# Maxima of the self attention's first group moved from the attention loop into the program before it

## Chip, cores and metric

One Trainium2 chip, one core in use. The metric is the device time of one execution in microseconds (us), median of several runs. The profile is that of one further execution.

## What is computed

The reference is a decoder of two post-normalised layers on `x` of 4 x 512 x 256. The part that matters here is the seam between the routed expert layer of layer 0 and the self attention of layer 1:

```python
x = _layernorm(x + _L0_ffn_ref(x, ...))            # 16 experts, top 1, plus a shared expert
x = _layernorm(x + _L1_attn_ref(x, L1_attn_wq_w, ...))
# _L1_attn_ref: 4 batches of 512 rows, 16 heads of 16 columns
q = apply_rope(x @ wq_w + wq_b); k = apply_rope(x @ wk_w + wk_b); v = x @ wv_w + wv_b
scores = einsum('bnqh,bnkh->bnqk', q, k) / sqrt(16)
scores = where(causal, scores, finfo.min)
attn = softmax(scores); ctx = einsum('bnqk,bnkh->bnqh', attn, v); out = ctx @ wo_w + wo_b
```

## The kernel before

**The combining program** (`combine_and_prepare`, from L1504) has 13 steps `c`. In steps 0 to 7 it adds the experts' outputs and normalises a chunk of x; in steps 2 to 9 the chunk is transposed; from step 4 on each step makes one pair of blocks: q or k of one batch, 128 columns by 512 rows each (16 blocks `n`, four for a batch, q before k). A block is projected by PE (L1591), rotated by DVE in two instructions of two parts (`dve_rot`, L333 and L334), added by POOL (`pool_whole`, L353) and then split in three bf16 parts, since the scores are made from bf16 products: ACT rounds it (`act_hi`, L318), DVE takes the rest (`dve_rest`, L342), ACT rounds that (`act_mid`, L325), POOL makes the third part (`pool_lo`, L358), and SP stores the parts to the HBM tensors `qs` and `ks` (L368). After the k blocks of a batch PE makes its values (L1599), ACT copies them (`val.act_copy`, L517) and SP stores them to `vs` (L523). Step 10 makes the q blocks of the last batch (12 and 13), step 11 its k blocks (14 and 15, called REST). DVE's list in a step is: rotate this step's blocks, then the rests of the step before. The splitting of blocks 14 and 15 and the stores of blocks 12 to 15 and of the last batch's values (`keys.late`) are left to the next program. SP loads Q and K of the first three groups of heads (`sa_Q`, `sa_K`) before the stores of blocks 6, 8 and 10.

**The attention loop** (`heads_loop(..., "sa", ...)`, from L1778) runs over 16 groups of 4 heads of one batch, with a ring of R = 5 buffers. For each group:
- phase 1: 16 units (head, 128 query rows). PE makes the scores of one unit (L1992) in one of 3 PSUM banks; DVE adds the causal mask and takes the row maximum into `mx` in one instruction (L2136), which frees the bank. 
- shift: DVE splits the maxima in two bf16 parts (`high` L2149, `low` L2153), PE turns them (L2001), DVE copies them to `mrow` (L2157), and two small DMAs of SP (`maxima`, L1878) put them as two more rows under Q. This stands behind unit 3 of the next group.
- phase 2: PE makes the transposed scores with the shift included (L2016, pairs of heads, two PSUM pair-banks), ACT takes Exp (L2091), POOL cuts the triangle (L1928), PE multiplies with the values (L2032), ACT copies the output (L2081).

The order on PE is: 16 units of group 0; 16 units of group 1, with shift(0) behind unit 3; then phase 2 of group 0, with the 16 units of group 2 strewn in, and so on: phase 2 of group g runs with phase 1 of group g+2. In the first group, units 0 to 4 of group 2 and shift(1) stand before the third pair of scores. DVE makes the two rests of blocks 14 and 15 behind units 4 and 6 of group 1. ACT waits for the landing of the last value store before its first Exp.

The order on SP in the loop is: stores of blocks 12 and 13; `maxima(0, 0)`; stores of block 14; value store and store of block 15; `stored` (a wait for all of these); loads of Q and K of groups 3 and 4; `maxima(1, 1)`; reload for group 5; `maxima(2, 2)`; and so on.

Of the kernel before, what the change touches and what calls it, by code (L numbers as in the profile page):

```python
# [27 lines left out]
F32 = mybir.dt.float32  # L28
BF16 = mybir.dt.bfloat16
I32 = mybir.dt.int32  # L30
ALU = mybir.AluOpType
ACT = mybir.ActivationFunctionType
AX = mybir.AxisListType.X

P = 128
B, L, D = 4, 512, 256
N = B * L
T = N // P
TB = L // P
# [9 lines left out]
G = 4  # L49
# [1454 lines left out]
def combine_and_prepare(nc, env, hT, xs, slot, hb):  # L1504
# [14 lines left out]
    with ExitStack() as c_:  # L1519
# [10 lines left out]
        def dst(n):  # L1530
# [5 lines left out]
        sp_ = Split(env, c_, "sqk", L, bias, dst, lambda n: [SLOTS[blocks[n][1]]], 4, homes=lambda n: HOMES[blocks[n][1]],  # L1536
                    rope=lambda n: (env.cos, env.sin_neg if blocks[n][2] == 0 else env.sin))

        pair = lambda item: PS[:, (4 + 2 * (item % 2)) * BANK:(6 + 2 * (item % 2)) * BANK]
        item_of = lambda n: 3 * (n // 4) + n % 4 // KD  # L1540

# [4 lines left out]
                pe.wait_ge(val.s_v, b + 1) if what == 2 else sp_.freed(pe, 4 * b + KD * what + 1)  # L1546

        def store(sp, n):
            if n % 4 == 3:
                val.sp_out(sp, n // 4)  # L1550
            sp_.sp_out(sp, n)

        with nc.Block() as block:

            @block.gpsimd
            def _(pool):
                def gather(c):
                    for t in PAIR_TILES(c):
                        pool.indirect_dma_start(out=xs[:, t, :], out_offset=None, in_=env.yg,
                                                in_offset=bass.IndirectOffsetOnAxis(ap=slot[:, t:t + 1], axis=0)  # L1560
                                                ).then_inc(s_ga[c], 16)

                for c in range(AHEAD):
                    gather(c)
                for c in range(STEPS):
                    if c < CHUNKS:
                        tail.pool_rstd(pool, c)
                    if c + AHEAD < CHUNKS:
                        gather(c + AHEAD)
                    for n in blocks_at(c):  # L1570
                        sp_.pool_whole(pool, n)
                    for n in blocks_at(c - 1):
                        if n not in REST:
                            sp_.pool_lo(pool, n)

            @block.tensor
            def _(pe):
                pe.sem_inc(tail.s_proj, DONE)
                for c in range(STEPS):
                    if DONE <= c < CHUNKS:  # L1580
                        tail.pe_proj(pe, c, lambda k: w["f_wd"][:, k, :],
                                     lambda i, k: hT[:, k, (2 * c + i) * P:(2 * c + i + 1) * P])
                    if 2 <= c < CHUNKS + 2:
                        tail.pe_out(pe, c - 2)
                    for n in blocks_at(c):
                        b, name, m = blocks[n]
                        if m == 0:
                            pe.wait_ge(tail.s_xT, TB // 2 * (b + 1))
                            item_free(pe, item_of(n))
                        for k in range(KD):  # L1590
                            last = pe.matmul(pair(item_of(n))[:, m * L:(m + 1) * L], w["s_w" + name][:, k, m * P:(m + 1) * P],  # L1591
                                             env.xT[:, k, b * L:(b + 1) * L], start=(k == 0), stop=(k == KD - 1))
                        last.then_inc(sp_.s_full, 1)
                        if n % 4 == 3:
                            item_free(pe, 3 * b + 2)
                            for j in range(TB):
                                t = b * TB + j
                                for k in range(KD):
                                    last = pe.matmul(pair(3 * b + 2)[:, j * D:(j + 1) * D], env.xT[:, k, t * P:(t + 1) * P],  # L1599
                                                     w["s_wv"][:, k, :], start=(k == 0), stop=(k == KD - 1))  # L1600
                            last.then_inc(val.s_full, 1)

            @block.scalar
            def _(act):
                for c in range(STEPS):
                    if 2 <= c < CHUNKS + 2:
                        tail.act_out(act, c - 2)
                    if len(blocks_at(c - 1)) and blocks_at(c - 1)[-1] % 4 == 3:
                        b = blocks_at(c - 1)[-1] // 4
                        val.act_copy(act, b, pair(3 * b + 2))  # L1610
                    for n in blocks_at(c - 1):
                        if n not in REST:
                            sp_.act_mid(act, n)
                    for n in blocks_at(c):
                        if n not in REST:
                            sp_.act_hi(act, n, None)

            @block.vector
            def _(dve):
                val.init(dve)  # L1620
                for c in range(STEPS):
                    if c < CHUNKS:
                        u = c % tail.ring
                        tail.dve_sum(dve, c, biased=False)
                        dve.wait_ge(tail.s_r, c + 1)
                        dve.wait_ge(s_ga[c], 16 * 2)
                        dve.tensor_tensor(tail.r[:, u, :, :], tail.r[:, u, :, :], xs[:, 2 * c:2 * c + 2, :],
                                          ALU.add).then_inc(s_all, 1)
                        tail.dve_stats(dve, c, ready=s_all)
                    if 1 <= c <= CHUNKS:  # L1630
                        tail.dve_apply(dve, c - 1)
                    for n in blocks_at(c):
                        m = blocks[n][2]
                        ps = pair(item_of(n))
                        sp_.dve_rot(dve, n, n - m + KD, ps[:, m * L:(m + 1) * L], ps[:, (1 - m) * L:(2 - m) * L])
                    for n in blocks_at(c - 1):
                        if n not in REST:
                            sp_.dve_rest(dve, n)

            @block.sync  # L1640
            def _(sp):
                def load(g):
                    hb.load_q(sp, g, g)
                    hb.load_k(sp, g, g)

                for n in range(LATE):
                    if n == LOADS[0]:
                        sp_.sp_end(sp, 4)
                    if n in LOADS:
                        load(LOADS.index(n))  # L1650
                    store(sp, n)

    return LaterKeys(sp_, val, store, range(LATE, len(blocks)), REST)

class LaterKeys:

    def __init__(self, split, val, store, late, rest):  # L1660
        self.split, self.val, self.store, self.late, self.rest = split, val, store, late, rest

    def landed(self, engine, b):

# [7 lines left out]
class HeadBuffers:  # L1672
# [5 lines left out]
    def __init__(self, env, c, name, NK, causal, qp, kp, vp, Q=None):  # L1678
# [3 lines left out]
        sb, _ = env.alloc(c)  # L1682
        self.K = sb(name + "_K", [P, self.RING, G * NK], BF16)
        self.Q = Q if Q is not None else sb(name + "_Q", [P, self.RING, G, L], BF16)

    def grow(self, env, c, name, ring):

# [87 lines left out]
    return units  # L1775

def heads_loop(nc, env, name, hb, OT, keys=None, queries=None):  # L1778

# [10 lines left out]
    cut = [0, NK] if causal else [0, BANK, 2 * BANK, NK - LEFT, NK]  # L1791
    CUTS = len(cut) - 1
    if causal:
        units = [(h + j, qt, 0) for h in range(0, G, 2) for qt in (3, 0, 2, 1) for j in range(2)]
    else:
        units = units_of_cuts(CUTS)
    U = len(units)
    R1 = 3
    EARLY = U if causal else 18
    LEAD = U if causal else 5  # L1800
    TURNS = 3
# [31 lines left out]
    with ExitStack() as c:  # L1833
# [2 lines left out]
        PR = KT if causal else R  # L1836
        Pr = sb(name + "_P", [P, PR, G, L], F32)
        part = sb(name + "_part", [P, 2, COLS, CUTS], F32)
        mx = sb(name + "_mx", [P, 2, COLS], F32)
        mh = sb(name + "_mh", [P, 2, 2, COLS // 2], BF16)  # L1840
        mrow = sb(name + "_mrow", [2 * COLS, P], BF16)
        if R > hb.RING:
# [3 lines left out]
        s_ones = sem(name + "_ones")  # L1846
        s_v = [sem(f"{name}_v{u}") for u in range(R)]
        s_mq = [sem(f"{name}_mq{u}") for u in range(R)]
        s_1 = sem(name + "_1")
        s_1free = sem(name + "_1free")  # L1850
        if not causal:
            s_cuts = sem(name + "_cuts")
            s_mrow = sem(name + "_mrow")
# [13 lines left out]
        with nc.Block() as block:  # L1867

            @block.sync
            def _(sp):  # L1870
# [13 lines left out]
                    hb.load_k(sp, g + R, u)  # L1884

                if causal:
                    for n in keys.late:
                        if n == keys.rest[0]:
                            maxima(0, 0)
                        keys.store(sp, n)  # L1890
                    keys.stored(sp)
                else:
                    hb.load_q(sp, 1, 1)
# [8 lines left out]
                    hb.load_q(sp, u, u)  # L1902
                    hb.load_k(sp, u, u)
                for g in range(GROUPS - 1):
                    maxima(g + 1, (g + 1) % R)
                    if g + R < GROUPS:
                        reload(g, g % R)

# [60 lines left out]
            def _(pe):  # L1969
# [93 lines left out]
                for n in range(U):  # L2063
                    if not causal and n in project_at:
                        block_, k = project_at[n]
                        queries.project(pe, block_, queries.ps(block_), (k,))
                    unit(0, 0, n, 0)
                for n in range(LEAD):
                    unit(1, 1, n, 0)
                    if n == BEHIND:  # L2070
# [7 lines left out]
            def _(act):  # L2078
# [23 lines left out]
                act.sem_inc(s_pv, PR)  # L2102
                act.sem_inc(s_ot, 1)
                if causal:
                    for n in keys.rest:
                        keys.split.act_hi(act, n, None)
                    for n in keys.rest:
# [16 lines left out]
            def _(dve):  # L2124
# [33 lines left out]

                for g in range(GROUPS):
                    for n in range(U):  # L2160
                        unit(g, n)
                        if causal and (g, n) in rest_after:
                            keys.split.dve_rest(dve, rest_after[g, n])
                        if not causal and not g and n in split_after:
# [590 lines left out]
```

## Time and profile before

| | us |
|---|---|
| median of 3 runs | 1492.09 |
| lowest and highest | 1489.83 and 1494.17 |
| the profiled execution, whole | 1491.71 |
| its span | 1489.7 |
| PE busy in the span | 1368.9 |
| DVE busy | 1062.0 |
| ACT busy | 774.5 |
| the combining program's last two steps, up to the loop's first matmul | 619 to 642 |
| the attention loop | 642 to 800 |

The busy time of PE is a poor guide here: matmuls are pipelined and overlap with waiting, and each stage of the kernel has its own limit. The stage to look at is read from the order of time: which engine starts what, and what it had waited for.

### The profile page before, as it was taken

The page shows a single profiled execution, that of the slowest core. Times are in us where ns is not written, and L with a number is a line of the kernel's source. Part 1 is how long each engine was busy: PE and PEld are TensorE (multiplying, and loading weights), DVE is VectorE, ACT ScalarE, POOL GpSimd, SP SyncE. Part 2 cuts the span into 40 slices and gives each one's busy share as a digit, 9 for nine tenths or more (in the row PEclk, how much of TensorE's full clock was granted, in tenths as well). Part 3 has the DMA queues.
Part 4 walks back from the last instruction along what each step waited for, and adds up shares of the span by engine and source line. Part 5 has one row for each costly group of instructions (what it writes and reads, how often), then busy time and mean ns, then how long its engine had stood idle before and what let it go on. Part 6 is the DMA issues. An engine that isn't in the chain of part 4 may idle for free. (4 is left out here: it accounts for less than half of the span.)

```text
span 1489.7 us, 24886 instructions
## 1 busy us (share of the span) xinstructions
PE 1368.9 (92%) x9358; PEld 761.6 (51%) x9358; DVE 1062.0 (71%) x2351; ACT 774.5 (52%) x1066; POOL 322.9 (22%) x407
## 2 busy tenths in 40 slices
PE   6897899989999989858998889999999999999996
PEld 3565578856898877423345422333333333333285
DVE  4887466661121128878994798999999999997077
ACT  2344266621111102326664315787888888888754
POOL 3110322243000017743335440000000000000011
PEclk9999799999999999959999968999999999999999
DMA  9548533356988842774421650333222343220001
GB/s 340 194 139 245 166 122 128 124 171 228 299 274 300 278 143 80 222 216 123 134 76 42 187 171 2 77 98 91 68 67 68 80 100 86 68 67 2 1 1 57
DMA packets 152841, 198.68 MB, mean 133 GB/s; under 512 B 15723, under 2 KB 124799, under 8 KB 152594
## 3 DMA queue, kind: packets, MB, share of 16 engines
q1 hardware_dynamic: 141004, 165.34, 36.9%
q0 software_dynamic: 9200, 29.64, 6.5%
q10 hardware_dynamic: 2518, 2.13, 0.5%
q8 instruction: 74, 1.21, 0.3%
q14 instruction: 45, 0.37, 0.1%
HBM read 136.08 MB, written 60.70 MB: 132 GB/s over the span
## 5 line engine op out<-in xcount | busy, mean ns | idle before, releaser
L2139 DVE TENSOR_REDUCE xa_part<-psum 128x1 f32<-128x512 f32 (+1 forms) x768 | 462.6, 661 | 20.5 <-PE psum L1992 18.6
L2091 ACT ACTIVATE xa_P<-psum 128x1024 f32<-128x1024 f32 (+1 forms) x416 | 403.5, 1020 | 105.4 <-PE psum L2016 104.7
L2016 PE MATMUL psum<-sa_Q,xa_K 48*128 48x512 bf16 (+3 forms) x1664 | 268.1, 382 | 3.9 <-DMA sa_Q<-xa_mrow 2.9
L1992 PE MATMUL psum<-xa_K,sa_Q 48*128 48x512 bf16 (+1 forms) x768 | 239.4, 388 | 4.9 <-DVE xa_part L2139 1.5
L2032 PE MATMUL psum<-xa_P,xa_V 128*32 128x512 f32 (+1 forms) x1664 | 223.5, 609 | 0.4 <-ACT xa_P L2091 0.4
L1992 PEld LDWEIGHTS psum<-xa_K,sa_Q 48*128 48x128 bf16 x768 | 59.3, 94 | 232.1 <-DVE xa_part L2139 160.6
L2016 PEld LDWEIGHTS psum<-sa_Q,xa_K 48*128 48x128 bf16 (+3 forms) x1664 | 105.7, 97 | 69.5 <-ACT xa_P L2091 21.2
L2136 DVE CUSTOM_DVE_ANT_0 psum<-psum,cf_sb 128x512 f32<-128x512 f32 (+3 forms) x256 | 119.4, 521 | 19.3 <-PE psum L1992 18.6
L1334 PEld LDWEIGHTS psum<-xtT,wgu 128*128 128x128 f32 x992 | 115.5, 192 | 5.8 <-issue 4.6
L1334 PE MATMUL psum<-xtT,wgu 128*128 128x128 f32 x992 | 115.9, 275 | 1.4 <-issue 0.8
L2091 ACT ACTIVATE sa_P<-psum 128x1024 f32<-128x1024 f32 (+3 forms) x128 | 83.4, 702 | 43.3 <-PE psum L2016 43.1
L1483 DVE TENSOR_TENSOR ht<-sgt,psum 128x512 f32<-128x512 f32 x31 | 21.3, 687 | 113.4 <-ACT sgt L1386 113.4
L1386 ACT ACTIVATE sgt<-psum 128x512 f32<-128x512 f32 x31 | 18.5, 597 | 132.7 <-PE psum L1334 132.7
L1992 PE MATMUL psum<-sa_K,sa_Q 48*128 48x512 bf16 (+3 forms) x256 | 70.6, 331 | 13.9 <-DVE sa_mx L2136 6.7
L212 POOL TENSOR_TENSOR t_rstd<-t_ve,mhalf 128x2 f32<-128x2 f32 (+1 forms) x36 | 27.6, 767 | 228.3 <-DVE t_ve L207 228.1
L2016 PE MATMUL psum<-sa_Q,sa_K 50*128 50x256 bf16 (+7 forms) x512 | 65.1, 311 | 4.8 <-ACT sa_P L2091 2.5
L1941 POOL CAST xa_mh<-xa_mx 128x16 bf16<-128x16 f32 x16 | 3.2, 198 | 295.0 <-DVE xa_mx L2145 266.9
L2032 PEld LDWEIGHTS psum<-xa_P,xa_V 128*32 128x32 f32 (+1 forms) x1664 | 33.0, 108 | 54.1 <-issue 50.6
L634 PE MATMUL psum<-a_in_sb,xT_sb 128*128 128x384 f32 x128 | 48.4, 525 | 12.6 <-DMA xT_sb<-in_xT 9.9
L1928 POOL TENSOR_SCALAR_AFFINE_SELECT sa_P<-sa_P 128x512 f32<-128x512 f32 x64 | 40.7, 636 | 87.7 <-ACT sa_P L2091 87.7
L1215 PE MATMUL psum<-xT_sb,big_weights 128*128 128x512 f32 x128 | 58.8, 614 | 0.6 <-PEq L937 0.6
L1344 PE MATMUL psum<-wdn,ht 128*128 128x256 f32 x248 | 58.7, 380 | 0.6 <-DVE yt L1490 0.6
(245 smaller groups left out, 2126.2 us busy)
## 6 DMA issues: line engine op xcount, KB each, us to landing
wgu<-in_f_gu SPq DMA_DIRECT2D x31, 1024.0 KB
xa_K<-kx SPq DMA_DIRECT2D x192, 100.1 KB, 5.0
wdn<-in_f_dn SPq DMA_DIRECT2D x31, 512.0 KB
vx<-xv_v SPq DMA_DIRECT2D x48, 256.0 KB, 3.4
xa_V<-vx POOLq DMA_DIRECT2D x16, 768.0 KB, 6.5
sa_Q<-qs SPq DMA_DIRECT2D x64, 96.0 KB, 2.3
sa_K<-ks SPq DMA_DIRECT2D x64, 96.0 KB, 2.4
sa_Q<-qx SPq DMA_DIRECT2D x64, 96.0 KB, 2.3
```

The costliest lines, as they stand in the source:

```text
L212: pool.tensor_tensor(self.rstd[:, u, :], self.ve[:, u, :], self.env.mhalf[:, 0:self.tc], ALU.pow).then_inc(self.s_rstd, 1)
L634: pe.matmul(o, env.xT[:, k, t * P:(t + 1) * P], w["a0_in"][:, k, cols], start=(k == 0), stop=False)
L1215: last = pe.matmul(o, w[name][:, k, f * P:(f + 1) * P], env.xT[:, k, c * L:(c + 1) * L], start=(k == 0), stop=(k == KD - 1))
L1334: last = pe.matmul(GU(j)[:, f * P:(f + 1) * P], wgu[:, u, k, f * P:(f + 1) * P], xtT[:, u, k, :], start=(k == 0), stop=(k == KD - 1))
L1344: last = pe.matmul(Y_PS[:, 0:D], ht[:, u, f, :], wdn[:, u, f, :], start=(f == 0), stop=(f == FC - 1))
L1928: pool.affine_select(square, square, [[0, G], [1, P]], ALU.is_ge, 0.0, base=0, channel_multiplier=-1).then_inc(s_tri, 1)
L1992: last = pe.matmul(out[:, 0:width], hb.q(u)[tile:tile + HALF, to, qt * P:(qt + 1) * P], hb.k(u)[tile:tile + HALF, to, cut[e]:cut[e] + widt ...
L2016: last = pe.matmul(out(j), hb.k(u)[tile:tile + depth, to, kt * P:kt * P + r], hb.q(u)[tile:tile + depth, to, q0(kt):L], start=(half == 0), ...
L2032: last = pe.matmul(O_PS[h * VW:(h + 1) * VW, q0(kt):L], Vg[0:r, u, kt, h * VW:(h + 1) * VW], Pr[0:r, (u * KT + kt) % PR, h, 0:L - q0(kt)], ...
L2091: act.activation(Pr[0:r, (u * KT + kt) % PR, h:h + 2, 0:w_], S_PS(p)[0:r, :, 0:w_], ACT.Exp, scale=SCALE).then_inc(s_exp, 1)
L2136: dve.tensor_tensor_reduce(src[:, 0:k1], src[:, 0:k1], env.later[:, L - k1:L], 1.0, -3e38, ALU.add, ALU.max, mx[:, g % 2, col + qt:col + q ...
L2139: dve.tensor_reduce(part[:, g % 2, col + qt, e:e + 1], src[:, 0:cut[e + 1] - cut[e]], AX, ALU.max).then_inc(s_1free, 1)
```

## The change

- Units 0 to 15 of group 0 are taken out of the loop, on PE and DVE, and put into the combining program as class `FirstMaxima`: units 0 to 7 at the end of PE's list for step 10, units 8 to 15 at the end of step 11 (behind the k blocks and the values). In DVE's list six of the eight stand between the rotations and the rests, two behind the rests. They use PSUM banks 0 to 2 and wait for the tail's transposes to be done, and for the load of group 0.
- `mx` is allocated with the head buffers, and the two semaphores of phase 1 in the combining program.
- SP in the loop: the last batch's value store goes first, ahead of the stores of blocks 12 and 13; `maxima(1, 1)` goes ahead of `stored` and the loads of groups 3 and 4.
- ACT in the loop: a one-element Exp goes first, so that the table of Exp is loaded there.

```diff
@@ combine_and_prepare
+        first = FirstMaxima(env, hb, sem)
+        units_at = lambda c: range((c - CHUNKS - 2) * first.STEP, (c - CHUNKS - 1) * first.STEP) if c in (CHUNKS + 2, CHUNKS + 3) else ()
         def store(sp, n):
-            if n % 4 == 3:
+            if n % 4 == 3 and n // 4 < B - 1:
                 val.sp_out(sp, n // 4)
@@ PE, end of a step
+                    for n in units_at(c):
+                        if n == 0:
+                            pe.wait_ge(tail.s_r, CHUNKS)
+                            pe.wait_ge(tail.s_xT, CHUNKS)
+                        first.pe_unit(pe, n)
@@ DVE, after the rotations
+                    for n in units_at(c)[:first.BEFORE_REST]:
+                        first.dve_unit(dve, n)
                     for n in blocks_at(c - 1):
                         if n not in REST:
                             sp_.dve_rest(dve, n)
+                    for n in units_at(c)[first.BEFORE_REST:]:
+                        first.dve_unit(dve, n)
@@
+CAUSAL_UNITS = [(h + j, qt) for h in range(0, G, 2) for qt in (3, 0, 2, 1) for j in range(2)]
+UNIT_BANKS = 3
+class FirstMaxima:
+    STEP = len(CAUSAL_UNITS) // 2
+    BEFORE_REST = 6
+    def pe_unit(self, pe, n):
+        h, qt = CAUSAL_UNITS[n]
+        if n == 0:
+            pe.wait_ge(self.hb.s_kq[0], 16 * self.hb.LOADS)
+        if n >= UNIT_BANKS:
+            pe.wait_ge(self.s_1free, n - UNIT_BANKS + 1)
+        tile, to, width = base(h), place(h, 0), (qt + 1) * P
+        pe.matmul(self.bank(n)[:, 0:width], self.hb.q(0)[tile:tile + HALF, to, qt * P:(qt + 1) * P],
+                  self.hb.k(0)[tile:tile + HALF, to, 0:width], start=True, stop=True,
+                  tile_position=(tile, 0)).then_inc(self.s_1, 1)
+    def dve_unit(self, dve, n):
+        h, qt = CAUSAL_UNITS[n]
+        dve.wait_ge(self.s_1, n + 1)
+        src, col, width = self.bank(n), h % 2 * G * TB // 2 + h // 2 * TB, (qt + 1) * P
+        dve.tensor_tensor_reduce(src[:, 0:width], src[:, 0:width], self.env.later[:, L - width:L], 1.0, -3e38,
+                                 ALU.add, ALU.max, self.hb.mx[:, 0, col + qt:col + qt + 1]).then_inc(self.s_1free, 1)
@@ heads_loop, SP
                 if causal:
+                    keys.val.sp_out(sp, B - 1)
                     for n in keys.late:
                         if n == keys.rest[0]:
                             maxima(0, 0)
                         keys.store(sp, n)
+                    maxima(1, 1)
                     keys.stored(sp)
@@
                 for g in range(GROUPS - 1):
-                    maxima(g + 1, (g + 1) % R)
+                    if g >= 1 or not causal:
+                        maxima(g + 1, (g + 1) % R)
@@ heads_loop, PE
-                    unit(0, 0, n, 0)
+                    if not causal:
+                        unit(0, 0, n, 0)
@@ heads_loop, ACT
                 if causal:
+                    act.activation(part[0:1, 0, 0, 0:1], env.mhalf[0:1, 0:1], ACT.Exp)
@@ heads_loop, DVE
-                        unit(g, n)
+                        if g or not causal:
+                            unit(g, n)
```

## Rows read from the trace of the kernel before

**Rows 1.** Timeline, outputs of the groups: start, length, engine, line, operation [idle before].
```profile
677.42 0.60 ACT L2081 ACTIVATE OT<-psum 128x512 f32<-128x512 f32 x1
687.90 0.60 ACT L2081 ACTIVATE OT<-psum 128x512 f32<-128x512 f32 x1
696.03 0.60 ACT L2081 ACTIVATE OT<-psum 128x512 f32<-128x512 f32 x1
```
**Rows 2.** Windows: length, busy of PE, PEld, DVE, ACT, POOL, granted clock, DMA share, GB/s.
```profile
622.60:627.20 4.60, 0.00 (x0) 0.00 (x0) 4.28 (x6) 1.74 (x4) 3.97 (x3) 0.77 0.92 266
627.20:632.00 4.80, 4.74 (x6) 2.17 (x7) 0.39 (x1) 1.44 (x3) 2.27 (x2) 0.50 0.95 295
674.90:685.30 10.40, 9.84 (x82) 3.61 (x84) 7.21 (x30) 5.76 (x9) 2.84 (x5) 0.67 0.34 100
685.30:695.50 10.20, 9.46 (x106) 4.08 (x102) 9.73 (x45) 6.98 (x11) 3.68 (x6) 1.00 0.50 139
```
**Rows 3.** Timeline of the combining program's end, and the loop's first matmul.
```profile
618.96 3.60 PE L1591 MATMUL psum<-xT_sb,s_wq_sb 128*128 128x512 f32 x8
...
627.26 6.00 PE L1591 MATMUL psum<-xT_sb,s_wk_sb 128*128 128x512 f32 x8 [4.70 <-ACT sv_v L517]
...
633.10 3.62 PE L1599 MATMUL psum<-s_wv_sb,xT_sb 128*128 128x256 f32 x16
...
635.94 2.35 DVE L342 TENSOR_TENSOR sqk_rest<-sqk_whole,sqk_parts 128x512 f32<-128x512 f32 x2
...
637.70 2.71 POOL L358 TENSOR_TENSOR sqk_parts<-sqk_rest,sqk_parts 128x512 bf16<-128x512 f32 x2
...
642.08 0.69 PE L1992 MATMUL psum<-sa_K,sa_Q 48*128 48x512 bf16 x3 [5.37 <-PEq L1553]
```
**Rows 4.** Timeline of DVE: first units of groups 0, 1 and 2, and shift(0).
```profile
642.70 0.70 DVE L2136 CUSTOM_DVE_ANT_0 psum<-psum,cf_sb 128x512 f32<-128x512 f32 x1 [4.41 <-PE psum L1992]
...
650.45 0.70 DVE L2136 CUSTOM_DVE_ANT_0 psum<-psum,cf_sb 128x512 f32<-128x512 f32 x1
...
652.37 0.28 DVE L2157 CAST sa_mrow<-psum 32x128 bf16<-32x128 f32 x1
...
660.88 0.70 DVE L2136 CUSTOM_DVE_ANT_0 psum<-psum,cf_sb 128x512 f32<-128x512 f32 x1 [0.28 <-PE psum L1992]
```
**Rows 5.** Timeline of the first groups' phase 2: scores, table load, Exp, shift rows.
```profile
659.38 1.24 PE L2016 MATMUL psum<-sa_Q,sa_K 50*128 50x512 bf16 x4
...
662.72 1.28 ACT L2091 ACT_TABLE_LOAD   x1 [5.64 <-DMA vs<-sv_v]
...
664.01 3.71 ACT L2091 ACTIVATE sa_P<-psum 128x1024 f32<-128x1024 f32 x4
665.09 0.82 PE L2016 MATMUL psum<-sa_Q,sa_K 50*128 50x384 bf16 x4 [1.27 <-ACT sa_P L2091]
...
674.89 0.61 PE L2016 MATMUL psum<-sa_Q,sa_K 50*128 50x512 bf16 x4 [2.22 <-DMA sa_Q<-sa_mrow]
```
**Rows 6.** Timeline of SP's issues in the loop: start, length of issuing, line, count.
```profile
642.04 2.06 SPq L368 DMA_DIRECT2D qs<-sqk_parts  x4
656.84 2.87 SPq L523 DMA_DIRECT2D vs<-sv_v  x4
672.45 1.27 SPq L1878 DMA_DIRECT2D sa_Q<-sa_mrow  x2
```
**Rows 7.** DMA: windows of three stretches, then both queues' shares in 646 to 648.
```profile
644.00:646.00 2.00, 1.38 (x5) 0.51 (x5) 1.90 (x11) 0.00 (x0) 2.00 (x4) 0.50 0.82 193
643.00:651.00 8.00, 5.12 (x16) 1.62 (x16) 7.80 (x33) 0.40 (x1) 3.34 (x5) 0.50 0.93 291
657.00:659.00 2.00, 1.28 (x5) 0.40 (x4) 1.91 (x9) 0.07 (x1) 1.79 (x2) 0.50 1.02 319
...
q1 hardware_dynamic: 398, 0.39, 55.5%
q0 software_dynamic: 111, 0.33, 46.8%
```

More of the change, by code:

```diff
@@ L1651, in _, with __init__ @@
                     store(sp, n)
-    return LaterKeys(sp_, val, store, range(LATE, len(blocks)), REST)
+    return LaterKeys(sp_, val, store, range(LATE, len(blocks)), REST, first)
 class LaterKeys:
-    def __init__(self, split, val, store, late, rest):
-        self.split, self.val, self.store, self.late, self.rest = split, val, store, late, rest
+    def __init__(self, split, val, store, late, rest, first):
+        self.split, self.val, self.store, self.late, self.rest, self.first = split, val, store, late, rest, first
     def landed(self, engine, b):
@@ L1684, in __init__ @@
         self.Q = Q if Q is not None else sb(name + "_Q", [P, self.RING, G, L], BF16)
+        self.mx = sb(name + "_mx", [P, 2, G * TB], F32)
     def grow(self, env, c, name, ring):
@@ L1775, in units_of_cuts, with __init__, bank @@
     return units
+CAUSAL_UNITS = [(h + j, qt) for h in range(0, G, 2) for qt in (3, 0, 2, 1) for j in range(2)]
[3 more added lines that the diff above has]
+    BEFORE_REST = 6
+    def __init__(self, env, hb, sem):
+        self.env, self.hb = env, hb
+        self.s_1 = sem("sa_1")
+        self.s_1free = sem("sa_1free")
+    def bank(self, n):
+        return self.env.PS[:, n % UNIT_BANKS * BANK:(n % UNIT_BANKS + 1) * BANK]
+    def pe_unit(self, pe, n):
[14 more added lines that the diff above has]
+                                 ALU.add, ALU.max, self.hb.mx[:, 0, col + qt:col + qt + 1]).then_inc(self.s_1free, 1)
 def heads_loop(nc, env, name, hb, OT, keys=None, queries=None):
@@ L1793, in heads_loop @@
     if causal:
-        units = [(h + j, qt, 0) for h in range(0, G, 2) for qt in (3, 0, 2, 1) for j in range(2)]
+        units = [(h, qt, 0) for h, qt in CAUSAL_UNITS]
     else:
@@ L1797, in heads_loop @@
     U = len(units)
-    R1 = 3
+    R1 = UNIT_BANKS
     EARLY = U if causal else 18
@@ L1838, in heads_loop @@
         part = sb(name + "_part", [P, 2, COLS, CUTS], F32)
-        mx = sb(name + "_mx", [P, 2, COLS], F32)
+        mx = hb.mx
         mh = sb(name + "_mh", [P, 2, 2, COLS // 2], BF16)
@@ L1848, in heads_loop @@
         s_mq = [sem(f"{name}_mq{u}") for u in range(R)]
-        s_1 = sem(name + "_1")
-        s_1free = sem(name + "_1free")
+        s_1 = keys.first.s_1 if causal else sem(name + "_1")
+        s_1free = keys.first.s_1free if causal else sem(name + "_1free")
         if not causal:
```

## The prediction

> **What bounds the kernel now.** I read first, in the timeline, when the outputs of the attention's groups come. From the second output on they are 8.13 us apart, but the first two are 10.48 us apart [rows 1]: the loop runs at its own pace only from group 2 on, and what stands ahead of that is a start-up. The windows say what sets the pace: in 685.3 to 695.5 DVE is busy for 9.73 of 10.20 us at a full granted clock, in 674.9 to 685.3 for only 7.21 of 10.40 at a mean clock of 0.67 [rows 2]. So DVE's unit instructions bound the steady loop, and start-up time is time in which DVE had nothing to do or did group 0 alone.
>
> Next the start-up, in order of time. PE does nothing from 622.6 to 627.3, since the k projection waits for a PSUM pair that ACT has still to copy [rows 3], and the clock falls to 0.50 for that projection [rows 2]: 6.00 us for it, where the same eight matmuls for q took 3.60 [rows 3]. The combining program ends on POOL at 640.41 and the loop's first matmul runs at 642.08. DVE makes group 0's units from 642.70 to 650.45 (7.75 us), then group 1's with the two late rests, and starts on group 2 at 660.88 [rows 4]. PE's first phase 2 scores come at 659.38, but Exp only at 664.01, because ACT waited for the last value store, issued at 656.84 [rows 6], and then loaded its table for 1.28 us [rows 5]. Last, group 1's scores wait 2.22 us for their shift rows [rows 5], which SP issued at 672.45, behind its loads [rows 6].
>
> **The change, part by part.** I call S the time of the loop's first instructions (642.04 now) and X that of its first scores (659.38 now).
>
> *Units 0 to 7, step 10.* DVE's rotations end at about 625.3, PE is idle until 627.26. By the 7.75 us for 16 units [rows 4], six take 3.0 us (four wide ones of 0.5 to 0.65, two of 0.25 us), so they end at 628.3, and the rests of blocks 10 and 11 move 2 to 3 us back; POOL and SP have room there, as SP issues loads until 633.9. PE can issue unit 7 only when unit 4 has left its bank, so the k projection starts at 628.3: +1.0 us.
>
> *The k projection.* A few short matmuls in a gap of nearly 5 us don't look like enough to hold the clock: the loop's start has the same kind of matmuls, more of them, at 0.50. I take 6.00 us again; the other bound is 3.60 [rows 3]. It ends at 634.3, the values (3.62 us) at 637.9, against 636.7 before.
>
> *Units 8 to 15, step 11.* They stand behind the values on PE. DVE starts them at 638.3, the first six end at 641.4, and only then come the rests of blocks 12 and 13 (2.35 us in the row, which lay beside POOL's work; I take 1.7): 643.1. In the trace POOL's last part ended 2.1 us after the rests did (638.29 and 640.41) [rows 3], and the program ends with it: 645.2, and with the same 1.65 us between the programs S = 646.8, 4.8 us later than now. With a full clock in the projection it is 644.4.
>
> *Loop, up to X.* With group 0 gone, PE gets to the first scores at S + 9.6 (group 1's units took it from DVE's 650.45 to 659.38, and DVE's first unit comes 0.65 us after S) [rows 4, 5]: 656.4. But the scores also need group 0's shift rows. SP now issues four value stores (2.87 us), four q stores (2.06) [rows 6] and then the shift rows, at S + 5.0. Shift(0) on DVE is done by S + 2.9, so it is not late; the queue is. The rows of data say how much: in 643 to 651 the DMA engines were busy for 0.93 and moved 2.3 MB (the q stores and POOL's five loads of V) [rows 7]; now 1.05 MB of values stand in front. At the 319 GB/s of 657 to 659, when such stores ran alone, this adds 3.3 us, and all is through at S + 12.1. The two queues shared the engines, 55.5% and 46.8% in 646 to 648 [rows 7], so I let the shift rows land with the end of the whole: X = 658.9. The lower bound is 656.4, the upper one goes by the 193 GB/s of 644 to 646 for all 3.4 MB: S + 18.6 = 665.4. I stay near the lower, as the mean row is 291.
>
> The Trainium skill (DMA: Bandwidth & Descriptors, "Issuing engines are not separate DMA queues") says that transfers from SP, ACT and POOL run on the same 16 engines and interleave. The trace agrees, by the two shares above. It speaks against this change: were SP's queue alone in its bandwidth, its 2.1 MB at 319 GB/s would be through at S + 7.7 and the shift rows hidden behind PE's S + 9.6, 2.5 us sooner.
>
> *Value store first, table first.* The values have landed by X at the latest, so neither the 5.64 us wait nor the table load stands ahead of Exp any more [rows 5]. Exp follows the first scores by some 0.7 us (an estimate: the first pair of matmuls at the half clock). The table load itself is worth nothing on top, since ACT would have had time for it before X. Its cover is the wait for the shift rows; without that it would cost 1.3 us.
>
> *From X to group 1's scores.* Now the third pair of scores goes at 665.09, and from there to the end of group 0's share is 7.6 us (672.7, where the wait of 2.22 starts) [rows 5]. With Exp ready, the third pair has only units 0 to 4 of group 2 before it, about 3 us behind X at the half clock. That gives X + 10.5 = 669.4, against 674.89: 5.5 us gained. DVE's own sum is not above it: S + 0.65, 10.0 for group 1 with the rests, 8.15 for group 2 and an idle 2.7 before X is 668.3.
>
> *Shift rows of group 1 ahead of the loads.* They are issued at about 662, needed at 669.4: the 2.22 us wait goes (its share is in the 5.5), and with it the idle that stands ahead of the fall to a clock of 0.67 [rows 2]. Group 1 should then run at near the steady 8.15 us and not 10.48 [rows 1]. What is late next: Q and K of group 3, issued from about 663.7 and landed at 669.7, and the shift rows of group 2, which now stand behind the loads of groups 3 to 5 on SP and can land at 677.2 with the scores due at 677.6. I give these two 0.3 us: 2.0 us gained.
>
> Sum: 5.5 + 2.0 = 7.5 us. All later stages follow their predecessors, so it stays. The profiled execution goes from 1491.71 to 1484.2; it lay 0.4 under the median, and the median goes from 1492.09 to **1484.6**.
>
> **The rivals.** *Early* (0.18): the units in the gap keep the clock up, or it rises sooner, and the projection takes 3.60: S is 2.4 us earlier, and the shift rows may land up to 2.4 before my sum. For it: PE has matmuls at both ends of the gap. Against it: 0.50 all through 642 to 651 in the wider rows [rows 7]. Gain 9.9 to 12.3: 1482 to 1480. *Eaten up* (0.24): something on SP's queue comes late (rows of group 2 behind three groups of loads, or the first shift rows at a mean rate of some 240 GB/s) and half or more is lost: gain 0.5 to 4.5, 1491.5 to 1487.6. For it: DMA shares of 0.92 to 1.02 all over this stretch [rows 2, 7]. *Slower* (0.08): the first shift rows behind 3.4 MB at 193 GB/s. X = 665.4 makes group 1's scores at 675.9, and as PE idles for 9 us first, the clock is low and group 1 keeps its 10.5: 1 us lost, 1493; if the second half's delay of POOL is also larger (the two rests at 2.35 and units at their bank-bound pace, 2 us), 1495, and 1497 with the loads of group 3 late. It decides from X = 664.4 on; below that it is a gain. *It does not do what it says*: the table is loaded at another place. It would change nothing, by the cover above.
>
> **How the numbers follow.** Forecast 0.50, with 1483 to 1487.5 as its own range. The measurement can tell about 0.3%, 4.5 us. Faster by more than that: nearly all of the forecast, all of early, none of eaten up: 0.66. Within it: 0.28, slower 0.06. The range of 1480.0 to 1491.0 leaves out the slower cases and the extreme of each side.
>
> **What would show it.** The loop's first instruction at 644 to 647; the k projection at 6.00 or 3.60; the first scores at 9.6 or 12 us behind the loop's start, and waiting for the shift rows; Exp less than 1 us behind them with the table load near the loop's start; no wait of group 1's scores; outputs 8.2 to 8.5 us apart from the first on. I am wrong if the loop starts after 649, if the first shift rows come more than 15 us behind the loop's start, or if the rows of group 2 are waited for.

## The result and the profile after

The changed kernel takes 1487.21 us in the median of 20 runs (1482.72 to 1489.52), the kernel before 1492.22 (1489.44 to 1494.49). The ratio is 0.9965, with a 95% interval of 0.9958 to 0.9973: 4.0 to 6.3 us faster. The profiled execution has a span of 1487.1 us, against 1489.7. The forecast was a gain of 7.5 us, to 1484.6; the measured time is inside its range of 1480.0 to 1491.0, and the gain of 5.0 us is a third smaller than forecast.

First, the end of the combining program and the loop's start in the trace after (start, length, engine, line, operation, [idle before <- what ended it]); it answers to [rows 3].

```profile
628.58 5.54 PE L1594 MATMUL psum<-xT_sb,s_wk_sb 128*128 128x512 f32 x8
...
640.76 1.29 DVE L342 TENSOR_TENSOR sqk_rest<-sqk_whole,sqk_parts 128x512 f32<-128x512 f32 x2
...
642.19 2.26 POOL L358 TENSOR_TENSOR sqk_parts<-sqk_rest,sqk_parts 128x512 bf16<-128x512 f32 x2 [3.97 <-ACT sqk_parts L325]
...
646.27 0.69 PE L2045 MATMUL psum<-sa_K,sa_Q 48*128 48x512 bf16 x3 [5.54 <-PEq L1556]
```

The k projection starts 1.3 us later and is still slow, the two rests of blocks 12 and 13 start at 640.8 instead of 635.9, POOL ends 4.0 us later with them, and the loop starts 4.0 us later (SP's first instruction; PE's first matmul 4.2). The windows (the granted clock is the seventh figure, before DMA share and GB/s) show that the clock still fell, though the units stood in the gap:

```profile
622.90:628.50 5.60, 1.80 (x9) 0.55 (x8) 5.46 (x15) 1.70 (x3) 3.64 (x3) 0.73 0.85 257
628.50:634.10 5.60, 5.60 (x10) 2.50 (x10) 2.15 (x8) 2.49 (x4) 2.26 (x2) 0.66 0.89 275
```

SP's issues, which answer to [rows 6]; L1928 is the shift rows:

```profile
646.08 2.35 SPq L523 DMA_DIRECT2D vs<-sv_v  x4
648.47 4.23 SPq L368 DMA_DIRECT2D qs<-sqk_parts  x4
652.75 2.35 SPq L1928 DMA_DIRECT2D sa_Q<-sa_mrow  x2
...
662.25 1.27 SPq L1928 DMA_DIRECT2D sa_Q<-sa_mrow  x2
663.79 1.75 SPq L1735 DMA_DIRECT2D sa_Q<-qs  x4
...
676.66 1.28 SPq L1928 DMA_DIRECT2D sa_Q<-sa_mrow  x2
```

And the first scores of the groups, with what they or their neighbours waited for, which answer to [rows 5]:

```profile
646.22 1.28 ACT L2159 ACT_TABLE_LOAD   x1 [2.59 <-PEq L1556]
...
658.53 1.04 PE L2069 MATMUL psum<-sa_Q,sa_K 50*128 50x512 bf16 x4 [2.31 <-DMA sa_Q<-sa_mrow]
...
659.68 1.02 ACT L2145 ACTIVATE sa_P<-psum 128x1024 f32<-128x1024 f32 x1 [6.17 <-PE psum L2069]
...
669.18 0.71 PE L2069 MATMUL psum<-sa_Q,sa_K 50*128 50x512 bf16 x4
...
670.58 0.39 PE L2045 MATMUL psum<-sa_K,sa_Q 48*128 48x512 bf16 x2 [0.69 <-DMA sa_K<-ks]
...
680.33 0.61 PE L2069 MATMUL psum<-sa_Q,sa_K 50*128 50x512 bf16 x4 [0.32 <-DMA sa_Q<-sa_mrow]
```

The scores start only 0.85 us sooner than before, 12.4 us behind the loop's start, since they wait for group 0's shift rows. Exp is 1.15 us behind them instead of 4.6. Group 1's scores are 5.7 us sooner. But group 1 itself takes 11.15 us to group 2's scores: its units wait for group 3's K, then the clock falls for 3.3 us, then group 2's rows are late.

```profile
673.40:676.70 3.30, 3.30 (x20) 0.83 (x18) 1.50 (x7) 1.51 (x2) 1.37 (x2) 0.50 0.65 205
680.30:688.50 8.20, 7.46 (x82) 3.20 (x84) 7.27 (x33) 5.69 (x9) 2.72 (x6) 1.00 0.43 129
```

The outputs, which answer to [rows 1]: 5.05, 5.03 and 4.93 us sooner, so most of what group 1's scores had gained (5.7 us) stays, and group 1's own share added nothing to it.

```profile
672.37 0.59 ACT L2135 ACTIVATE OT<-psum 128x512 f32<-128x512 f32 x1
682.87 0.60 ACT L2135 ACTIVATE OT<-psum 128x512 f32<-128x512 f32 x1
691.10 0.60 ACT L2135 ACTIVATE OT<-psum 128x512 f32<-128x512 f32 x1
```

### The profile page after: what moved, and what is told of

Read it like the earlier page. It is cut to its first block and busy times, and to the rows that moved or that the text cites. A ratio compares the mean times of both kernels' runs of the same rounds, so it can differ in the third digit from the quotient of the medians.

```text
span 1487.1 us, 24888 instructions
## 1 busy us (share of the span) xinstructions
PE 1369.3 (92%) x9358; PEld 762.8 (51%) x9358; DVE 1059.4 (71%) x2351; ACT 774.8 (52%) x1067; POOL 321.7 (22%) x407
## 5 line engine op out<-in xcount | busy, mean ns | idle before, releaser
L2045 PEld LDWEIGHTS psum<-xa_K,sa_Q 48*128 48x128 bf16 x768 | 59.2, 94 | 232.5 <-DVE xa_part L2194 160.8
L2191 DVE CUSTOM_DVE_ANT_0 psum<-psum,cf_sb 128x512 f32<-128x512 f32 (+1 forms) x240 | 111.5, 520 | 18.3 <-PE psum L2045 17.5
L2045 PE MATMUL psum<-sa_K,sa_Q 48*128 48x512 bf16 (+1 forms) x240 | 64.7, 321 | 12.1 <-PEq L1556 5.5
L634 PE MATMUL psum<-a_in_sb,xT_sb 128*128 128x384 f32 x128 | 48.5, 526 | 12.9 <-DMA xT_sb<-in_xT 10.1
```

Of the source, the lines that this page charges most:

```text
L634: pe.matmul(o, env.xT[:, k, t * P:(t + 1) * P], w["a0_in"][:, k, cols], start=(k == 0), stop=False)
L2045: last = pe.matmul(out[:, 0:width], hb.q(u)[tile:tile + HALF, to, qt * P:(qt + 1) * P], hb.k(u)[tile:tile + HALF, to, cut[e]:cut[e] + widt ...
L2191: dve.tensor_tensor_reduce(src[:, 0:k1], src[:, 0:k1], env.later[:, L - k1:L], 1.0, -3e38, ALU.add, ALU.max, mx[:, g % 2, col + qt:col + q ...
```

## The experiments

The table counts all times of one profile from the start of its last q projection (618.96 before, 619.31 after), so that what lies ahead of the changed stretch drops out. Columns: the loop's start on SP; first scores of groups 0, 1, 2 and 3; last output of the loop; then the time from there to the end of the span; the median and the ratio to the kernel before, with its interval. The runs were made on several chips, on which the kernel before took 1491.3 (e1 to e4), 1493.1 (e5 to e8) and 1492.5 us (e9 to e12), so kernels are compared by their ratios and not by their medians. 0.0010 of the ratio is 1.5 us.

| kernel | loop | sc. 0 | sc. 1 | sc. 2 | sc. 3 | last out | rest | median | ratio |
|---|---|---|---|---|---|---|---|---|---|
| before | 23.1 | 40.4 | 55.9 | 66.3 | 74.4 | 180.0 | 690.7 | 1492.2 | |
| after | 26.8 | 39.2 | 49.9 | 61.0 | 69.2 | 174.9 | 692.8 | 1487.2 | 0.9965 (0.9958-0.9973) |
| e1 orders only | 23.1 | 40.4 | 52.3 | 62.0 | 72.8 | 178.5 | 692.0 | 1491.0 | 0.9989 (0.9978-1.0001) |
| e2 units only | 26.7 | 36.6 | 53.6 | 64.1 | 72.3 | 177.8 | 693.4 | 1491.2 | 0.9999 (0.9990-1.0008) |
| e3 rows 0 first | 26.6 | 36.9 | 48.5 | 58.0 | 67.7 | 173.4 | 688.8 | 1483.1 | 0.9946 (0.9932-0.9959) |
| e4 rests first | 23.7 | 36.4 | 47.0 | 57.4 | 65.6 | 171.3 | 692.8 | 1485.4 | 0.9959 (0.9945-0.9972) |
| e5 orders, rows 2 first | 23.0 | 40.4 | 52.2 | 60.7 | 68.8 | 174.6 | 693.2 | 1488.1 | 0.9968 (0.9956-0.9980) |
| e6 rows 0 and 2 first | 26.7 | 36.6 | 47.4 | 56.2 | 64.4 | 170.1 | 690.2 | 1481.6 | 0.9925 (0.9910-0.9940) |
| e7 e4 and e6 together | 23.8 | 33.9 | 45.5 | 54.0 | 62.1 | 167.9 | 693.2 | 1481.3 | 0.9921 (0.9908-0.9935) |
| e8 eight matmuls | 28.0 | 41.0 | 52.3 | 61.7 | 71.4 | 177.1 | 688.8 | 1487.4 | 0.9961 (0.9947-0.9976) |
| e9 three matmuls | 26.3 | 38.6 | 49.4 | 59.2 | 67.3 | 173.0 | 691.4 | 1485.6 | 0.9953 (0.9937-0.9970) |
| e10 rows 1 late | 26.7 | 38.9 | 52.8 | 63.0 | 71.1 | 176.9 | 690.2 | 1488.0 | 0.9971 (0.9960-0.9982) |
| e11 no early table | 26.3 | 38.8 | 49.6 | 59.7 | 67.9 | 173.5 | 689.1 | 1485.0 | 0.9960 (0.9945-0.9974) |
| e12 e7 and three matmuls | 23.4 | 34.0 | 45.1 | 53.3 | 61.4 | 167.2 | 693.1 | 1480.1 | 0.9918 (0.9900-0.9937) |

**e1 and e2: each half of the change alone.** e1 is the kernel before with only the loop's orders of the change (three added lines; the conditions that take the same steps out of their old places are left out here):

```diff
+                    keys.val.sp_out(sp, B - 1)      # out of store(), ahead of the late stores
+                    maxima(1, 1)                    # ahead of keys.stored(sp)
+                    act.activation(part[0:1, 0, 0, 0:1], env.mhalf[0:1, 0:1], ACT.Exp)
```

> The kernel before with the loop's new orders alone (last value store first, shift rows of group 1 ahead of the loads, Exp table first); group 0's maxima stay in the loop. Theory A (the order on SP carries the gain): the loop starts at 642 as before, first scores at 659.4, Exp 0.7 us behind them instead of 4.6, group 1's scores at 669.9 without a wait for shift rows, against 674.9 before and 669.2 in the changed kernel: 4.5 us faster than before, about 1487.7. Rival B (the moved maxima carry the gain): at most 1.5 us faster than before, 1490.7 or more.

e2 is the changed kernel with these three undone.

> The changed kernel with the loop's old orders: only group 0's maxima are moved. Theory A: the loop starts at 646, first scores at 655.7, but the value store, issued behind the k blocks' parts, lands at about 660 and the table load follows, so Exp comes at 661.3; group 1's shift rows are issued behind the loads at about 669 and waited for until 671.4. 3.5 us faster than before, about 1488.7, so the two halves overlap and don't add up. Rival B: 4.5 us or more faster, below 1487.7. Rival C (the move alone is worth nothing, since the loop starts 4 us later): 1491 or more.

Neither half alone is clear of no change, and together they give 5 us. Up to group 2's scores e1 goes the way theory A said, if less far: group 1's scores come 3.6 us sooner than before and group 2's 4.3, where 5.0 was expected of group 1's. Group 2's scores wait for shift rows that stand on SP behind the loads of groups 3, 4 and 5. Behind that wait the clock falls, and group 2 takes 10.75 us, where in the kernel before it takes 8.1 (the timeline's row, then the window's).

```profile
682.73 0.61 PE L2019 MATMUL psum<-sa_Q,sa_K 50*128 50x512 bf16 x4 [1.17 <-DMA sa_Q<-sa_mrow]
```
```profile
685.00:691.20 6.20, 5.99 (x36) 2.13 (x40) 4.11 (x18) 3.25 (x6) 1.98 (x3) 0.50 0.22 57
```

In e2 the scores come 3.8 us sooner, and ACT waits longer than ever, 7.45 us, for the value store. Group 1's scores wait for their rows as before.

```profile
661.09 1.28 ACT L2142 ACT_TABLE_LOAD   x1 [7.45 <-DMA vs<-sv_v]
...
673.16 0.90 PE L2066 MATMUL psum<-sa_Q,sa_K 50*128 50x512 bf16 x4 [1.30 <-DMA sa_Q<-sa_mrow]
```

Theory A said 4.5 and 3.5 us and is wrong as it was put: it had the right waits up to group 1's scores, 1.4 and 1.5 us too early, and did not follow the chains to group 3's. Rival B, that the moved maxima carry the gain, has its number in e1 (at most 1.5 us) but not in e2, where it wanted 4.5 us or more, so it is out. Rival C, that the move alone is worth nothing, agrees with e2's median; its profile ends the loop 2.2 us sooner, and that is not seen in the median.

**e5 and e6: shift rows of group 2 ahead of the reload.**

```diff
+                if causal:
+                    maxima(2, 2)
                 for g in range(GROUPS - 1):
-                    if g >= 1 or not causal:
+                    if g >= 2 or not causal:
                         maxima(g + 1, (g + 1) % R)
```

On top of e1:

> The kernel of the orders alone, with one step more on SP: shift rows of group 2 ahead of the reload for group 5. Theory E (what the start-up gains is given back where a later group waits about 1 us for rows that are queued on SP behind loads, and the clock falls to 0.50 after the wait): no wait of group 2's scores, 9.7 us from them to group 3's become 8.2 to 8.5, so that 2 to 2.6 us of the lost gain come back: 1488.6 against 1491.0 for the orders alone. Rival F (group 2 is slow because its data are late on the DMA engines, whatever the order): within 0.8 us of the orders alone.

Group 2 takes 8.15 us, at a full clock, and the last output comes 3.9 us sooner than in e1. The ratio goes from 0.9989 to 0.9968, some 3 us; the two intervals just touch. Rival F is out, by the trace above all: no wait for rows is left and the group has its full pace. What is more, e5 moves no unit at all, and its ratio is that of the whole change (0.9968 and 0.9965). What the moved maxima add to e5's orders was not run.

```profile
679.00:687.20 8.20, 7.57 (x87) 3.30 (x85) 7.73 (x36) 5.69 (x9) 3.30 (x6) 1.00 0.69 187
```

On top of e3 (below):

> The kernel with group 0's shift rows ahead of the q stores (1483.05), with group 2's shift rows also ahead of the reload for group 5. Theory E: the 1.2 us wait of group 2's scores and the fall of the clock behind it go, group 2 takes 8.2 us instead of 9.6: 1.5 to 2.5 us faster, 1481.0. Rival F: within 0.8 us.

The ratio goes from 0.9946 to 0.9925 (the intervals overlap), and the last output comes 3.3 us sooner. Group 2 takes 8.2 us instead of 9.6, and group 1, which was thought not to change, 8.8 instead of 9.6, as its end no longer waits for group 2's rows. The remaining 1.1 us come before any of this, between the first scores and group 1's, where the clock rose sooner in this profile. One wait is left, for group 3's K, and the clock does not fall behind it (the timeline's row, then the window's):

```profile
667.32 0.39 PE L2046 MATMUL psum<-sa_K,sa_Q 48*128 48x512 bf16 x2 [0.43 <-DMA sa_K<-ks]
```
```profile
666.20:675.00 8.80, 7.66 (x85) 3.14 (x81) 7.75 (x36) 5.79 (x9) 3.24 (x5) 1.00 0.53 157
```

**e3: group 0's shift rows ahead of the q stores.**

```diff
                     keys.val.sp_out(sp, B - 1)
+                    maxima(0, 0)
                     for n in keys.late:
-                        if n == keys.rest[0]:
-                            maxima(0, 0)
```

> The changed kernel with group 0's shift rows issued directly behind the last value store, ahead of the stores of q blocks 12 and 13. The first scores should come at 9.6 us behind the loop's start instead of 12.4 (655.7 against 658.5) in every theory. Theory A (the start-up is bound by the DMA engines' data as a whole): the loads of group 3 still start at 663.8 and land at 670.5, units of group 3 wait for them for 3 us more, and less than 1 us is left: 1486.4 to 1487.2. Rival D (the late first scores are the whole bound): 2.8 us faster than the changed kernel, 1484.4.

The first scores come 2.3 us sooner, where all theories had 2.8. Theory A, that the loads of group 3 would eat this up, is too low: group 1's scores are 1.4, group 2's 3.0 us sooner, and no wait for group 3's K is left. Then group 2 meets the same wait and fall as e1, and half of it is lost again: the last output is 1.5 us sooner than in the changed kernel. By the ratio e3 is 2.8 us faster, which is rival D's number, but the trace up to the loop's end does not show so much; the rest of that profile behind the loop was 4 us shorter. The two lines are again a row of the timeline and one of the windows:

```profile
678.53 0.61 PE L2068 MATMUL psum<-sa_Q,sa_K 50*128 50x512 bf16 x4 [1.16 <-DMA sa_Q<-sa_mrow]
```
```profile
681.00:684.40 3.40, 3.40 (x20) 1.02 (x20) 2.33 (x11) 2.18 (x4) 1.01 (x2) 0.50 0.15 43
```

**e4: the rests of blocks 12 and 13 ahead of units 8 to 15.** In step 11 `BEFORE_REST` is 0 instead of 6.

> The changed kernel with the rests of blocks 12 and 13 ahead of units 8 to 15 on VectorE in step 11, so that GpSimd's last parts are not held up. The program should end on VectorE at 642.1 and not on GpSimd at 644.5, and the loop start 2.3 us earlier (643.8 against 646.1), its stores, first scores and loads all with it. Theory: 2.3 us faster than the changed kernel, 1484.9. Rival: the loads or the clock take it back, less than 0.8 us faster.

The rests start at 637.83 in a trace whose last q projection starts at 620.39, 1.1 us later than in the changed kernel's, so they are 4.0 us sooner by the table's count, and POOL ends 3.2 us sooner. The loop starts 3.1 us sooner, and the first scores, the groups and the last output go with it (2.8 to 3.6 us). By the ratio only 0.9 us of the expected 2.3 are seen, nearer to the rival's less than 0.8, and the intervals of this kernel and the changed one overlap: the trace shows the gain inside the loop, the times do not settle it.

```profile
637.83 2.35 DVE L342 TENSOR_TENSOR sqk_rest<-sqk_whole,sqk_parts 128x512 f32<-128x512 f32 x2
...
639.60 2.71 POOL L358 TENSOR_TENSOR sqk_parts<-sqk_rest,sqk_parts 128x512 bf16<-128x512 f32 x2
...
644.10 2.36 SPq L523 DMA_DIRECT2D vs<-sv_v  x4
```

**e7: e4 and e6 together.**

> The changed kernel with the three steps together: rests of blocks 12 and 13 ahead of units 8 to 15, group 0's shift rows ahead of the q stores, group 2's ahead of the reload for group 5. If they add up, 2.3 for the rests on top of the run with both rows first: 1479. If the loads of group 3 bound the start (they stand behind all stores), the rows bring less than 1 us on top of the rests alone: 1482 or more.

In the profile the loop ends 2.2 us before that of e6, but the ratios (0.9921 and 0.9925) don't tell the two apart: 0.6 us where 2.3 were expected if the steps add up, so in the measured times they are not shown to. The loads of group 3 are not waited for, so the expected reason is not the one. It is 6.5 us (0.0044) faster than the changed kernel and 11.8 (0.0079) faster than the one before, clear of both.

**e8, e9 and e12: is the k projection's length the clock?** Matmuls whose result nobody reads are put into PE's gap, to keep it busy:

```diff
                         first.pe_unit(pe, n)
+                        if n == UNIT_BANKS - 1:
+                            for _i in range(8):          # 3 in e9 and e12
+                                pe.matmul(PS[:, 3 * BANK:4 * BANK], w["s_wq"][:, 0, 0:P], env.xT[:, 0, 0:L], start=True, stop=True)
```

> The changed kernel with eight more 512-column float32 matmuls (into an unused bank, read by nobody) on TensorE between units 2 and 3 in step 10, so that the engine is busy in the gap ahead of the k projection. They cost 3.5 us of its idle time, which is 2.9 us there, so the projection starts up to 0.6 us later. Theory G (the projection's 5.5 us are the fallen clock): it takes 3.6 us, the loop starts 1.2 to 1.9 us earlier, 1485.6. Rival H (the gap doesn't matter, the clock falls anyway or other things set the program's end): within 0.5 us of the changed kernel, or slower.

> The changed kernel with three added 512-column float32 matmuls between units 2 and 3 in step 10 (each 0.9 us by the run with eight, 2.7 us together, in an idle time of 3.1 us), read by nobody. Theory G: the k projection starts as before at 9.3 us behind the start of the last q projection and takes 3.6 us instead of 5.5, the loop starts 1.9 us earlier, and as stores, first scores and loads all move with it, 1.5 to 2 us faster than the changed kernel, 1485.5. Rival H: the clock falls all the same, since short units stand on both sides, and nothing changes.

> The kernel with the three steps together (rests first, both shift rows first), with the three added matmuls of theory G as well. If they still move the loop's start: 1.5 us faster than without, 1479.7. If the start is then bound by the stores and loads of the DMA engines, which are busy up to the program's end, less than 0.7 us.

One such matmul takes 0.9 us, not 0.44, so eight of them are 7.1 us. In e8 the projection then takes 3.70 us at a clock of 1.00, and theory G has its cause right; but the projection starts 3.1 us later, and the loop 1.2 us, so that no time is gained (0.9961). The three of e9 fill 2.8 us of the gap and aren't enough: in the 2.2 us of units behind them PE is busy for 1.19, the clock falls, and the projection takes 5.40. Its median of 1485.6 is what theory G forecast, but by luck, since neither the short projection nor the earlier loop (0.5 us, not 1.9) came; the trace puts 1.4 us of it in group 1, which ran at a full clock. e12 is the same on top of e7, again with 5.40, and no verdict between them.

```profile
631.86 3.70 PE L1594 MATMUL psum<-xT_sb,s_wk_sb 128*128 128x512 f32 x8
```
```profile
632.00:634.00 2.00, 2.00 (x5) 0.91 (x6) 2.00 (x8) 1.31 (x3) 0.61 (x1) 1.00 0.75 214
```
```profile
626.40:628.60 2.20, 1.19 (x5) 0.46 (x5) 2.20 (x11) 1.54 (x2) 0.94 (x1) 1.00 0.82 211
628.60:634.00 5.40, 5.40 (x10) 2.36 (x10) 2.21 (x8) 2.49 (x4) 2.27 (x2) 0.68 0.91 278
```

The first two blocks of lines are e8, the third e9. In e9 group 2's scores wait 1.01 us for their rows, about as long as in e8 (0.92), and here the clock does not fall behind the wait:

```profile
678.79 0.61 PE L2072 MATMUL psum<-sa_Q,sa_K 50*128 50x512 bf16 x4 [1.01 <-DMA sa_Q<-sa_mrow]
```
```profile
680.00:682.00 2.00, 1.42 (x21) 0.76 (x20) 1.98 (x12) 1.93 (x3) 0.49 (x1) 1.00 0.63 196
682.00:684.00 2.00, 2.00 (x23) 0.77 (x21) 1.54 (x7) 1.51 (x2) 0.34 (x2) 1.00 0.06 14
```

**e10: group 1's shift rows behind the loads again.**

> The changed kernel with group 1's shift rows behind the loads of groups 3 and 4 again, as in the kernel before. By the queue they are issued at about 671.5 and land at 673.5, while the scores are due at 669.2: a wait of 4 us with a fall of the clock behind it, but the loads start 1.5 us sooner, so that group 3 is not waited for. 3 to 4.5 us slower than the changed kernel, 1490 to 1491.5. If the wait only takes the place of the one for group 3's K, less than 1.5 us slower.

Group 1's scores wait 2.88 us and come 2.9 us later than in the changed kernel, the last output 1.9 us later. The intervals of the two overlap; by their middles it is 0.9 us slower, where 3 to 4.5 were expected. The loads start sooner here, so group 1's units don't wait for K, and a part of the loss comes back.

```profile
673.25 0.61 PE L2067 MATMUL psum<-sa_Q,sa_K 50*128 50x512 bf16 x4 [2.88 <-DMA sa_Q<-sa_mrow]
```

**e11: no early table load.** The line of the one-element Exp is left out.

> The changed kernel without the one-element Exp ahead of the loop's ScalarE work. ScalarE has nothing to do for 6 us before the first scores (658.5), so the table load fits there, before its first real Exp: within 0.6 us of the changed kernel. Rival: the table load comes only with the first scores and costs its 1.28 us.

```profile
657.58 1.28 ACT L2145 ACT_TABLE_LOAD   x1 [6.13 <-PE psum L2069]
658.88 1.94 ACT L2145 ACTIVATE sa_P<-psum 128x1024 f32<-128x1024 f32 x2
661.00 1.59 ACT L2145 ACTIVATE sa_P<-psum 128x768 f32<-128x768 f32 x2 [0.18 <-PE psum L2069]
```

ACT was idle for 6.13 us and did not load the table in that time: the load came with the first scores, at 657.58, and the first Exp is 1.3 us later, as the rival said. Yet it costs nothing. The third Exp comes 4.56 us behind the first scores (656.44), in the changed kernel 4.55, because PE has five units and a shift to do before the third pair of scores. The ratio, 0.9960, is not told apart from the changed kernel's.

## Why the prediction was right or wrong

- **What bounds the start-up.** Right. Of the three gaps it named, two gave the gain (Exp behind the value store, group 1 behind its rows). The third, idle PE ahead of the k projection, took the units in and gave none: the loop starts later.
- **The combining program.** Right in mechanism, 0.8 us too late in size: the loop starts 4.0 us later by the clock of the trace (3.7 by the table's count), not 4.8. The k projection starts at 628.58 as worked out (628.3). It took 5.54 and not 6.00, and the rests 1.29 instead of 1.7. The low bound for it, a held clock, did not come; 7.1 us of matmuls in the gap held it (e8), 2.8 us did not (e9).
- **First scores.** Right: they wait for group 0's shift rows behind the value and q stores, 12.4 us behind the loop's start (12.1 was worked out from the GB/s rows). e3 shows the cause, by moving the rows: 10.3 us. That the size came out so well is in part luck: SP issued the rows 6.7 us behind the loop's start and not 5.0, as the q stores took 4.23 us to issue instead of 2.06, and the DMA engines moved 3.8 MB up to the scores and not 3.4, at 302 GB/s. The rule of the Trainium skill (DMA: Bandwidth & Descriptors, "Issuing engines are not separate DMA queues") leads to this longer time, since POOL's loads of V share the engines; a queue with the whole rate for itself would have given 9.6 by the prediction's estimate. The trace agrees as far as both queues were at work at once, with 64.1% and 31.1% of the engines' time in 646 to 659; no run takes one of them away.
- **Value store first.** Right in kind: Exp comes 1.15 us behind the scores, not 0.7, and no longer waits for the value store. The reason given for the table load's worth of nothing was wrong (it doesn't use the wait, e11), the worth was right, for another cause.
- **From the first scores to group 1's.** Right: 10.65 us against 10.5, group 1's scores at 669.2 against 669.4.
- **Group 1 at the steady pace, 2.0 us gained.** This is the step that failed. Group 1 takes 11.15 us, more than the 10.38 before, so that this term is 0.8 us lost and not 2.0 gained. The prediction named the two things that are late next, K of group 3 and rows of group 2, and gave them 0.3 us. Their waits are 0.69 and 0.32 us, 1.0 together. Left out altogether is a new fall of the clock: between the two waits PE ran for 3.3 us at 0.50. The prediction took the fall in the kernel before as the consequence of the 2.22 us wait alone, to go with it. The other runs bear out that it hangs on such waits, and not on their length alone. With no wait for rows or K from group 1's scores on, every group ran at 1.00 (e5, e7 and e12). Behind a wait of 0.9 to 1.2 us for group 2's rows the clock fell in e1, e3 and e8, and the group took 10.75, 9.64 and 9.67 us instead of 8.15; in e2 it was 10.46 us behind 1.30 for group 1's rows. The wait itself lies ahead of these times, in the group before. But in e9 it stayed at 1.00 behind a wait of 1.01 us. Behind a wait for group 3's K it fell in the changed kernel (0.69), e4 (0.36) and e11 (0.41), and stayed in e6 (0.43). So a wait can bring the fall and need not; what decides was not found, and no run takes out the wait for K alone.
- **All later stages follow.** In the mean yes: 5.08 us at the loop's last output, 5.0 in the median. In one execution no: the span of the profiled one is only 2.6 us shorter, see below.
- The rivals: "eaten up" is nearest to what happened to the last third of the gain, at one of the places it named; its own gains, 0.5 to 4.5 us, are smaller than the measured 5.0.
- The signs that it set for itself point the same way. The loop's start, the k projection (5.54 us, nearer to 6.00), the first scores and group 1's scores came as they should; Exp and the outputs' spacing (10.5 us once more behind the first) did not, and the rows of group 2 were waited for, which it had called a sign of being wrong.
- A part that nobody had asked: which edit carries the gain. Neither alone; and e5 has it without the moved maxima, by one more step of order. The start-up is a chain of waits on SP's queue, and taking 7.75 us of DVE's work out of it brought the changed kernel's first scores 0.85 us forward (by the trace's own clock).

## What to carry to other kernels

Where a start-up is bound by one issuing queue, ask of every small transfer on it which large ones stand ahead, and put those that an engine is about to wait for first; here the order on SP alone (value store first, shift rows of groups 1 and 2 ahead of the loads, with the early Exp: e5) brought what the whole change did. Follow a gain to the place where the loop is steady, since behind a wait of about 1 us in a matmul stage the clock cost 1.5 to 2.6 us more in four runs of five (e1, e2, e3, e8, and not e9). Two edits on one chain can each be worth next to nothing alone, so test them together as well.

## What the runs showed of the hardware

- From the loop's last output to the end, the same instructions in the same order took from 688.8 to 693.4 us in the 14 profiles (the table's column "rest"), which is more than several of the edits are worth. It goes with the clock just behind the loop: in the kernel before, PE kept 1.00 in the ten microseconds behind the last output, after the change 0.83. In the seven profiles with 0.83 there the rest was 692.0 us or more, in the seven with 1.00 it was 691.4 or less. Why one execution keeps the clock there and another doesn't was not tried. It may be a part of why the same kernel's runs spread over 7 us. One profile can't tell edits of 2 us apart at its end; the loop's own end, counted from a point ahead of the edit, can better.

The first line is the kernel before, the second the kernel after.

```profile
799.00:809.00 10.00, 7.76 (x49) 6.68 (x50) 4.96 (x15) 1.77 (x3) 5.67 (x6) 1.00 0.01 2
```
```profile
794.30:804.30 10.00, 8.01 (x37) 6.47 (x38) 3.76 (x12) 1.15 (x2) 4.43 (x6) 0.83 0.01 2
```

- The table load waits with the instruction that needs it: 6.13 us of idle ACT ahead of it were not used (e11). A one-element Exp that waits for nothing drew the load to the loop's start (646.22 in the changed kernel).
- A float32 matmul with 512 columns took 0.89 us at a clock of 1.00 and stands in the trace as two instructions (e8: eight of them are 16 rows of the profile and 7.13 us).
